# Gather masks with four experts innermost, and eight products of zeros ahead of the gather

## What is computed

```python
logits = jnp.einsum('bsd,de->bse', x, gate_w)          # 8 experts
affinity_T = jnp.transpose(softmax(logits), (0, 2, 1))
gating, index = jax.lax.top_k(affinity_T, K)            # K = 128 tokens per batch and expert
x_sel = x[b_idx, index]                                 # the gather
g = einsum('bekd,edi->beki', x_sel, Wg); u = einsum('bekd,edi->beki', x_sel, Wu)
out = einsum('beki,eid->bekd', silu(g) * u, Wd)
x_out = zeros_like(x).at[b_idx, index].add(out * gating[..., None])
```

## Time and profile before

| | |
|---|---|
| median of three runs | 518.32 us |
| span of the profiled execution | 516.1 us |
| the profiled execution's own time | not recorded apart; the median is 2.2 us over its span |
| TensorE busy | 427.1 us, 83% of the span |
| VectorE busy | 400.4 us, 78% |
| ScalarE busy | 239.9 us, 46% |
| masks, L746 | 32 instructions, 36.5 us busy |
| gather, L999 | 128 products, 53.7 us busy |
| facts, L1006 | 256 products of 5 columns |

### The profile page before, as it was taken

The page is one execution under the profiler, slowest core; times in us unless marked ns, Lnnn a source line. Parts: engine busy times, 40 slices in busy tenths (PEclk is TensorE's granted clock), DMA queues, the critical chain, the costliest instruction groups (busy, mean ns, idle before and its releaser), DMA issues.

```text
span 516.1 us, 7820 instructions
## 1 busy us (share of the span) xinstructions
PE 427.1 (83%) x2252; PEld 250.8 (49%) x2252; DVE 400.4 (78%) x841; ACT 239.9 (46%) x439; POOL 68.6 (13%) x105
## 2 busy tenths in 40 slices
PE   2605999995588899999999999999996506999995
PEld 2501557773454445555555545554553402567773
DVE  6698848899689987778777777777655598768884
ACT  2400443330341267777676777766784201543332
POOL 5510002149000010000000000000002500001100
PEclk9999999998788799999999999999999655999999
DMA  5000012210058810111111111110110000012212
GB/s 166 1 0 1 1 30 62 61 31 0 4 213 276 297 61 25 37 37 43 42 42 42 42 42 42 42 42 1 35 31 0 0 0 2 1 33 59 61 32 81
DMA packets 24749, 26.03 MB, mean 50 GB/s; under 512 B 3634, under 2 KB 16438, under 8 KB 24726
## 3 DMA queue, kind: packets, MB, share of 16 engines
q1 hardware_dynamic: 24726, 25.74, 16.0%
HBM read 16.16 MB, written 9.44 MB: 50 GB/s over the span
## 4 chain that ended last, share of the span: by engine, by line
PE 69%; DVE 25%; issue 3%; ACT 2%; DMA 1%; DVEq 0%; ACTq 0%
PE ps L1133 12%; PE ps L1158 12%; PE ps L1148 10%; DVE neg_max L807 6%; PE ps L999 5%; PE ps L1035 5%; DVE heads_out L707 3%; PE ps L1018 3%; PE ps L1020 3%; PE ps L1019 3%; DVE values L704 3%; PE ps L1050 2%; PE ps L1051 2%; PE ps L960 2%; DVE probs L746 2%
## 5 line engine op out<-in xcount | busy, mean ns | idle before, releaser
L807 DVE TENSOR_REDUCE neg_max<-ps 128x1 f32<-128x512 f32 x256 | 163.4, 684 | 38.9 <-PE ps L1133 38.9
L597 ACT ACTIVATE probs<-ps 128x512 f32<-128x512 f32 x256 | 137.8, 598 | 64.6 <-PE ps L1148 62.9
L1133 PE MATMUL ps<-k_stack,q_stack 128*128 128x512 f32 x256 | 113.7, 452 | 4.8 <-DVE neg_max L807 3.5
L1148 PE MATMUL ps<-q_stack,k_stack 128*128 128x512 f32 x256 | 100.6, 403 | 0.2 <-ACT probs L597 0.2
L1133 PEld LDWEIGHTS ps<-k_stack,q_stack 128*128 128x128 f32 x256 | 49.0, 192 | 68.8 <-DVE neg_max L807 61.7
L1158 PE MATMUL ps<-probs,v_ext 128*32 128x512 f32 x512 | 68.2, 605 | 0.0
L1148 PEld LDWEIGHTS ps<-q_stack,k_stack 128*128 128x128 f32 x256 | 47.7, 190 | 12.7 <-ACT probs L597 5.7
L523 ACT CAST k_stack<-ps 128x512 fp32r<-128x512 f32 x32 | 17.2, 589 | 67.7 <-PE ps L999 67.7
L451 POOL TENSOR_TENSOR w_lo<-w_gu,w_hi 128x512 fp32r<-128x512 f32 x16 | 20.4, 1279 | 149.7 <-ACT w_hi L510 149.7
L769 DVE TENSOR_TENSOR vae_and_gates<-heads_out,ps 128x512 f32<-128x512 f32 x32 | 21.9, 687 | 19.7 <-ACT heads_out L531 17.7
L746 DVE TENSOR_TENSOR probs<-slot_row,slot 128x1024 f16<-128x1024 f16 x32 | 36.5, 1216 | 0.1
(11 more groups left out here) (151 smaller groups left out, 574.8 us busy)
## 6 DMA issues: line engine op xcount, KB each, us to landing
parts_dram<-part_hi SPq DMA_DIRECT2D x8, 512.0 KB, 3.6
parts_dram<-part_lo SPq DMA_DIRECT2D x8, 512.0 KB, 4.9
q_stack<-parts_dram SPq DMA_DIRECT2D x32, 128.0 KB
k_stack<-parts_dram SPq DMA_DIRECT2D x32, 128.0 KB
w_gu<-in_L_ffn_Wg_dram SPq DMA_DIRECT2D x16, 128.0 KB, 2.1
w_gu<-in_L_ffn_Wu_dram SPq DMA_DIRECT2D x16, 128.0 KB, 2.2
wd_sb<-in_L_ffn_Wd_dram SPq DMA_DIRECT2D x16, 128.0 KB, 2.2
x<-in_L_attn_x_dram SPq DMA_DIRECT2D x4, 256.0 KB, 3.8
```

Of the source, the lines that this page charges most:

```text
L597: nc.scalar.activation(probs[:, u // HG, u % HG, :], ps[:, RING + ring_bank(step, u), :], ACT.Exp, scale=SCORE_SCALE).then_inc(probs_ready, 1)
L807: nc.vector.tensor_reduce(neg_max[:, g, qt, col:col + 1], ps[:, ring_bank(step, u), :], AX.X, ALU.max, negate=True).then_inc(max_taken, 1)
L1133: nc.tensor.matmul(ps[:, ring_bank(step, u), :], q_stack[:, g, pp, chunk(qt)], k_stack[:, g, 2 * pp + jj, :], start=True, stop=True).then_ ...
L1148: nc.tensor.matmul(ps[:, RING + ring_bank(step, u), :], k_stack[:, g, j, chunk(c)], q_stack[:, g, j // 2, :], start=True, stop=True).then_ ...
```

## The change

`slot_row` gets a fourth of a mask's experts as an inner dimension: 128 slot numbers, each four times, so 512 elements. `pick` is laid out in memory as [b, c, h, s, q], where the expert is 4h + q: the four experts of a half lie innermost. A mask instruction now walks h, s, q with q innermost, so that in all three of its operands neighbouring elements of the walk are neighbours in memory, where before the slot operand repeated one element 128 times. It still has 1024 elements per partition. TensorE reads a mask in the same order as before (expert, then slot), and so with a step of 4 elements of 2 bytes: as the moving operand of the gather, 512 columns, and as the weights of the facts, 128 columns. Before, both were contiguous.

Apart from that, TensorE runs eight products of 512 columns of `zeros` into the first bank of the gather, behind the counting of the marks and ahead of the waits of the gather, in each expert layer.

```diff
-        slot_row = sb("slot_row", [P, K], F16)
+        EQ = 4
+        slot_row = sb("slot_row", [P, K, EQ], F16)
...
-        pick = probs[:].rearrange("p k c s -> p (k c s)").bitcast(F16).rearrange("p (b c e s) -> p b c e s", b=B, c=C, e=E)
+        pick = probs[:].rearrange("p k c s -> p (k c s)").bitcast(F16).rearrange("p (b c h s q) -> p b c h q s", b=B, c=C, h=E // EQ, q=EQ)
...
+        WARM_UP = 8
...
-            nc.gpsimd.iota(slot_row[:], pattern=[[1, K]], base=1, channel_multiplier=0,
+            nc.gpsimd.iota(slot_row[:], pattern=[[1, K], [0, EQ]], base=1, channel_multiplier=0,
...
-                        nc.vector.tensor_tensor(pick[:, b, c], slot_row[:].unsqueeze(1).broadcast_to([P, E, K]),
-                                                slot[:, c, b * E:(b + 1) * E].unsqueeze(2).broadcast_to([P, E, K]),
+                        of_slot = slot[:, c, b * E:(b + 1) * E].rearrange("p (h q) -> p h q", q=EQ)
+                        nc.vector.tensor_tensor(pick[:, b, c].rearrange("p h q s -> p h s q"),
+                                                slot_row[:].unsqueeze(1).broadcast_to([P, E // EQ, K, EQ]),
+                                                of_slot.unsqueeze(2).broadcast_to([P, E // EQ, K, EQ]),
                                                 ALU.is_equal).then_inc(pick_ready[l], 1)
...
                 last.then_inc(marks_counted[l], 1)
 
+                for _ in range(WARM_UP):
+
+                    nc.tensor.matmul(ps[:, pick_bank(0), :], zeros[:, 0:P], zeros[:], start=True, stop=True)
                 if l == 0:
                     pe.wait_ge(rot_ready, 2)
...
-                                last = nc.tensor.matmul(ps[:, pick_bank(n) + k, :], half[:, C * b + c, :], pick[:, b, c, 4 * hf:4 * hf + 4, :],
+                                last = nc.tensor.matmul(ps[:, pick_bank(n) + k, :], half[:, C * b + c, :], pick[:, b, c, hf],
...
-                            last = nc.tensor.matmul(ps[:, 1, col:col + 5], pick[:, b, c, e, :], facts[:, c, b, e, :], start=(c == 0), stop=(c == C - 1))
+                            last = nc.tensor.matmul(ps[:, 1, col:col + 5], pick[:, b, c, e // EQ, e % EQ, :], facts[:, c, b, e, :], start=(c == 0), stop=(c == C - 1))
```

## The result

The changed kernel takes 545.03 us (median of four runs, 543.28 to 545.92), the kernel before 518.34 us in the same session. The ratio is 1.051, with a 95% interval of 1.049 to 1.054: 5% slower, where 513.1 us and a gain of 1% were forecast. The profiled execution took 543.28 us and its span is 541.6 us, 25.5 over the span before.

What follows compares the result with a forecast made beforehand. TensorE's gather was taken to become the bound, VectorE's masks being the slower before; gains of 2.46 and 2.74 us a layer sum to 5.2, so 518.3 - 5.2 = 513.1 us, range 511.5 to 516.

Steps and rivals of the forecast that it cites:

- I take 0.2153: Gather on TensorE: a strided product at full clock is spaced 0.2153 us, bounded above by 0.43.
- theory B: Follow-up forecast for the gather's products at a 32-byte step: bytes walked over set the cost, 1.80 us each, about 712 us.
- Rival A: Gather product's moving operand (L1007): the step halves the column rate, 0.4275 us a product, 538.8 us; chance 0.13.
- The facts' loads: TensorE loading masks as weights with a step of 8 bytes: 25 ns each, unchanged; upper bound 0.121 us.
- Rival B: Loading masks as weights for the facts: the step costs up to 0.121 us a load, 536.5 us; chance 0.10.
- The sum: Both layers' gathers: last product at 62.38 in the first, gains 2.46 + 2.74 = 5.2 us, span 510.9 us.
- the 0.54 for the low clock: Start of each layer's gather: 1.08 us run cold at half the work, so 0.54 us lost.
- Masks: VectorE's mask instructions: two elements per step, 0.69 us instead of 1216 ns, one every 0.61 us.
- Zeros: Eight TensorE products ahead of the gather: 3.42 us cold, from 42.41 to 45.83 in the first layer.
- The clock: TensorE's clock rises 4.5 us after the products of zeros start, at 46.91 in the first layer.
- The larger slot_row: Building 512 elements takes 0.56 and not 0.24 us, hidden by GpSimd's idle 3.28 us.

## Why the prediction was wrong

**The step that failed** is "I take 0.2153" for a strided product, and with it the reason: "because those products also load 4-byte weights, which the gather does not". The contiguous product with 4-byte operands at 0.23 us needs no weights to explain it. Its 512 columns fill 128 lines, and at 1.76 ns that is 0.226 us, the spacing of the step of 4 bytes, whose weights are the 2-byte ones of the gather: the read of the moving operand, seen at the point where it just exceeds the clock. (No run changed the width of the weights alone; that they add nothing is inferred.) I had the row that shows the limit, and laid it to something else. A moving operand of 16-bit elements, contiguous, needs 64 lines and hides the read. Had I divided bytes by time there (2048 in 0.23 us), a step of 8 bytes, which passes over 4096, would have come out at 0.46, though beyond 16 bytes the same division fails (theory B).

**Rival A** was what happened. I gave it 0.13 and 538.8 us; it was 545.0. Its mechanism was right (the product's moving operand), its size was not, because I took the halved column rate, 0.4275, as the end of the range. Measured was 0.451: 63 x 0.024 = 1.5 us a layer more. The facts add 0.8 a layer, and the last product, 0.63 us long and not 0.38, 0.25; in two layers these are 5.1 of the 6.2 us between 538.8 and 545.0. That the end of a range happened to be near was luck; at 16 bytes it is 0.90. It was built from the two rates of a clock that has no part in it.

The rule that I weighed there from the Trainium skill ("SBUF — State Buffer", the note on cachelines: lines of 16 bytes, full rate with at least two hits on a line) holds in the unit and fails in the threshold. The line of 16 bytes is what the runs show. But two columns to a line gave half rate, four columns 0.226 us, nearly full; the measurement decides. I let it stand as "by that rule this rival does not happen", and it weighed too much in the 0.13.

**The facts' loads.** Taken at 25 ns, measured at 33: 0.26 us a group, 0.8 a layer on the path. Rival B was right in kind and small. It was ranked beside A, but a load loses far less by a step than a product: with a line for every column, 128 columns as weights take 60 ns with their small product, and 512 as the moving operand 900.

**The sum.** Last product at 62.38 forecast, 77.51 measured, 15.13 apart: 63 x (0.451 - 0.2153) = 14.85, less the 0.54 for the low clock, which cost nothing here, plus 3 x 0.26 = 0.78, plus 0.04 for the start: 15.13. Two layers make 30.3 of the 30.7 us by which the span exceeds the 510.9 forecast; the rest is about the 0.25 us a layer of the longer last product.

**What was right.** Masks: 0.69 us forecast, 689 ns measured, mean of 32, and they come faster than TensorE takes them. This is the row that the trace of before lacked. It agrees with the rule that the prediction cites for it from the Trainium skill ("Vector Engine (DVE) Microarchitecture Reference", section 5.1): 16-bit operands with neighbours side by side go two at a time. Zeros: 42.41 to 45.83 forecast, 42.47 to 45.87 measured. The clock: 4.5 us after their start forecast, 445.8 - 440.5 = 5.3 us in the second layer (a mean of 0.61 from 445 to 446). That 4.5 was near is in part luck: in the kernel with two experts innermost and contiguous products, the gather's first product, 3.3 us after the first of the zeros, is already at full pace. The larger slot_row cost nothing that shows. The working of the gain was right as well: products contiguous, everything else as in the change, gave 513.84 where the forecast for the whole was 513.1, even with 0.8 us a layer of dearer facts.

## What to carry to other kernels

Before a layout is changed for one engine's sake, price the read on the other: count how many 16-byte lines an instruction of TensorE must pass and take 1.76 ns for each; 512 16-bit columns may have a step of up to 4 bytes. If the fast writer wants an interleaved layout, let TensorE read in the order of memory and undo the order where a copy out of PSUM has to be made anyway, with the step on the PSUM side. And a warm clock is worth only what the bound leaves of it: the same eight products of zeros gave nothing with slow masks, nothing with slow reads, and 1.8 us once neither was the bound.

## What the runs showed of the hardware that I had not expected

A TensorE that counts as busy without a pause can lose its clock. These are windows of the changed kernel, in the first layer's gather:

```profile
54.00:56.00 2.00, 2.00 (x15) 1.00 0.00 0
...
57.00:58.00 1.00, 1.00 (x4) 0.50 0.00 0
...
61.00:62.00 1.00, 1.00 (x21) 1.00 0.00 0
```

The busy share is 1.00 all the time, yet the granted clock falls to 1.2 GHz at about 56.7 and comes back at 60, and it falls once more from 63.5 to 66.9. The busy share doesn't show that a product's columns at full clock would need only 0.215 of each 0.451 us. With a step of 16 bytes the clock falls soon and stays low for the rest of the gather (the stretch from 482 to 540 above), and with 32 and 256 bytes it does not rise in the gather at all. What makes it fall was not tried.

It costs the strided products nothing, since they don't follow the clock, but what comes behind them can start slowly: with the 32-byte step the first expert's products are 0.43 us apart.

```profile
109.94 0.63 PE L1019 MATMUL ps<-k_stack,w_hi 128*128 128x512 f32 x1
110.37 0.63 PE L1020 MATMUL ps<-k_stack,w_lo 128*128 128x512 f32 x1
```

The window over these two reads a clock of 1.00, and it should not be believed: the trace's record of the clock begins with its first rise, here at 113.1, and what lies ahead of it reads 1.00. The second layer, where the record is there, has the same spacing:

```profile
540.00:543.00 3.00, 3.00 (x8) 0.50 0.00 0
```

ScalarE's copy out of PSUM costs nothing more at a step of 16 bytes (two in 1.07 us). Two took 1.92 us in the kernel with the 32-byte step, and there it is the side of SBUF that costs: those copies read PSUM in the order of memory and write `picked_hi` and `picked_lo` with a step of 16 elements, 64 bytes. With 256 bytes it is the other way round, PSUM read with a step of 16 bytes and SBUF written in order, and two take 1.07 us.
